# Token rows turned on TensorE, gathers first, and the weights loaded in three groups

## The reference

```
h = embed_matrix[x]                                   # x: (4, 1024) int32, embed_matrix: (50257, 192)
h = h + mamba_like(layernorm(h))                      # x@W_in, causal conv of 3, silu, cumsum*BC + xc*D, *silu(z), @W_out
h = h + routed_block(layernorm(h), ...)               # scores, 15% of the tokens attend, the others mix, then an FFN
h = h + memory_attention(layernorm(h), ...)           # 12 heads over the tokens and over 100 memory rows, gate alpha
h = h + ternary_ffn(layernorm(h), w1, g1, w2, g2)     # bitlinear -> gelu -> bitlinear
```

```
BC  = sum(B * C, axis=-1)
mkv = memory_features @ w_mem + b_mem                 # memory keys and values
weight_quant(w) = clip(round(w * s), -1, 1) / s,  s = 1 / max(mean(|w|), 1e-5)      # w1: (768, 192), w2: (192, 768)
```

## Time and profile before

| | us |
|---|---|
| median of 3 runs | 1982.28 |
| the runs | 1982.28, 1982.16, 1995.48 |
| the profiled execution | 1991.73 |
| its span, first to last instruction | 1989.9 |
| mean granted TensorE clock (share of full speed) | 0.878 |
| busy: PE, DVE, ACT, POOL | 1642.2, 1356.8, 971.2, 126.8 |

### The profile page before, as it was taken

One profiled execution on the slowest core, in us unless ns is written; L12 is line 12 of the kernel. 1 busy time (PEld: TensorE's weight loads), 2 busy tenths in 40 slices (PEclk: granted clock), 3 DMA queues, 4 the chain that ended last, 5 costly groups with the idle time before them and its releaser, 6 DMA issues.

```text
span 1989.9 us, 26444 instructions
## 1 busy us (share of the span) xinstructions
PE 1642.2 (83%) x9798; PEld 919.7 (46%) x9798; DVE 1356.8 (68%) x3076; ACT 971.2 (49%) x1383; POOL 126.8 (6%) x165
## 2 busy tenths in 40 slices
PE   0769878998999999964457898799999999999454
PEld 0348646654333333363243584656534333336323
DVE  4668663046889989677768477422588998984876
ACT  0422452124777777732532324330567777775153
POOL 5010000000000000005020100000000000000200
PEclk9977796998999999986568787899989999999656
DMA  6003210016010010001010312000510100100001
GB/s 149 1 1 112 68 44 0 1 35 187 25 32 25 25 32 25 1 1 32 0 33 0 99 45 67 13 0 1 179 60 25 32 25 27 30 9 1 0 0 32
DMA packets 53894, 73.39 MB, mean 37 GB/s; under 512 B 18712, under 2 KB 27205, under 8 KB 53767
## 3 DMA queue, kind: packets, MB, share of 16 engines
q1 hardware_dynamic: 52150, 68.54, 11.9%
q0 software_dynamic: 1616, 3.16, 0.7%
HBM read 38.51 MB, written 33.17 MB: 36 GB/s over the span
## 4 chain that ended last, share of the span: by engine, by line
PE 64%; DVE 26%; ACT 4%; issue 3%; DMA 2%; SPq 1%; POOL 0%; DVEq 0%; ACTq 0%
PE PV L905 9%; PE ST L889 8%; PE S L855 6%; PE ST L801 4%; PE ST L556 4%; PE MT L855 3%; PE PV L914 2%; DVE nmp L1529 2%; DVE Er L1605 2%; DVE st L1402 2%; PE S L812 2%; DVE R L1625 2%; DVE amax L1626 2%; PE ST L586 1%; PE S L850 1%
## 5 line engine op out<-in xcount | busy, mean ns | idle before, releaser
L1232 ACT ACTIVATE Er<-ST 128x1024 f32<-128x1024 f32 x384 | 377.1, 1021 | 106.2 <-PE ST L889 105.9
L1581 DVE TENSOR_REDUCE nmp<-S 128x1 f32<-128x512 f32 x514 | 337.7, 683 | 30.5 <-PE S L855 30.5
L889 PE MATMUL ST<-QS,KS 100*128 100x512 bf16 x768 | 218.0, 385 | 0.3
L905 PE MATMUL PV<-Er,V 128*17 128x512 f32 x1536 | 212.1, 602 | 0.0
L855 PE MATMUL S<-KS,QS 96*128 96x512 bf16 x514 | 183.3, 392 | 0.8
L1581 DVE TENSOR_REDUCE nmp<-MT 128x1 f32<-128x512 f32 x254 | 173.6, 683 | 13.5 <-PE MT L855 13.5
L855 PEld LDWEIGHTS S<-KS,QS 96*128 96x128 bf16 x514 | 48.2, 98 | 154.9 <-DVE nmp L1581 107.2
L450 POOL TENSOR_SCALAR tp<-mv 128x8 f32<-128x8 f32 x20 | 5.2, 258 | 1693.1 <-DVE mv L1406 1693.1
L1529 DVE TENSOR_REDUCE nmp<-S 128x1 f32<-128x512 f32 x120 | 77.5, 684 | 48.3 <-PE S L671 48.1
L889 PEld LDWEIGHTS ST<-QS,KS 100*128 100x128 bf16 x768 | 72.1, 99 | 64.2 <-ACT Er L1232 5.7
L855 PE MATMUL MT<-KS,QS 96*128 96x512 bf16 x254 | 99.4, 391 | 0.9 <-DVE nmp L1581 0.9
(11 more groups left out here) (386 smaller groups left out, 3210.9 us busy)
## 6 DMA issues: line engine op xcount, KB each, us to landing
KS<-scr_k SPq DMA_DIRECT2D x72, 192.0 KB, 2.7
scr_k<-R SPq DMA_DIRECT2D x16, 576.0 KB, 4.0
QS<-scr_q SPq DMA_DIRECT2D x48, 192.0 KB, 2.8
scr_k<-R SPq DMA_DIRECT2D x16, 384.0 KB, 4.6
QS<-scr_k SPq DMA_DIRECT2D x24, 192.0 KB, 2.4
scr_q<-R SPq DMA_DIRECT2D x8, 576.0 KB, 4.5
scr_k<-R SPq DMA_DIRECT2D x16, 192.0 KB, 5.2
scr_q<-R SPq DMA_DIRECT2D x8, 384.0 KB, 4.7
```

The costliest lines, as they stand in the source:

```text
L889: ins = nc.tensor.matmul(ST[i % 2][:, (kt % 2) * HALF:(kt % 2 + 1) * HALF], KS[0:KP + 4, k, kt * P:(kt + 1) * P], QS[0:KP + 4, k, half * H ...
L905: ins = nc.tensor.matmul(PV[row:row + VC, :], slots[h // H].V[:, kt, h % H, :], E[:, step % RING, (kt % 2) * HALF:(kt % 2 + 1) * HALF], st ...
L1232: A_(E[:, g, :], ST[i % 2][:, :], ACT.Exp).then_inc(s["exps"], 1)
L1581: v.tensor_reduce(nmp[:, u // 2, u % 2:u % 2 + 1], bank, AX.X, ALU.max).then_inc(s["reduced"], 1)
```

## The change

The change reorders the start of the kernel and one step of each pair.

- **Tokens.** SP loads the token numbers first, as 32 rows of 128 numbers. DVE turns the integers into floats, PE turns the 32 x 128 tile (with `ident`), and DVE writes the result as integers into `tok_i`. POOL waits for that and issues the gathers before most of its constants: eight for a, five for z, then a's inverse deviation, then z's last three and z's inverse deviation, then the remaining constants (`late_consts`).
- **Loads.** There are three semaphores: `early` (memory features, memory weight, w1, w2), `loaded` (input projection, convolution, columns, B and C) and `rest` (all others). PE waits for `early` before the memory products, for `loaded` before the first input projection, for `rest` before the first output projection.
- **Staging.** w1 and w2 are staged in the two buffers HS, and the memory weight in the buffer Er, in place of slot a's X, R and XT.
- **DVE.** Some of POOL's fills (vm, memt, splm, ones) and those of two PSUM banks are put at the start of DVE's list. Slot a's statistics come first; the split of the memory keys and w1's ternary passes stand between them and a's normalisation, w2's ternary passes before z's statistics. The fill of ksm, the rows of ones in XT and B*C (`late_fills`) stand between the first convolutions and the first scans.
- **Ternary weights.** PE turns them after the input projection of pair 0, in the four banks of D2, and ACT evicts them after the last SiLU of the convolution; PE waits for that (`wprep`) before the output projection.
- **Order within a pair, both pairs.** PE: turn a, project a (first half), turn z, project z; ACT accordingly.

```diff
-        wmem = slots[0].XT
-        w1 = slots[0].X[:, 0:FC, :]
-        w2 = slots[0].R[0:CH, 0:2 * F].rearrange("p (t f) -> p t f", t=2)
+        wmem = Er[0:CH + 1, 2720:2720 + 4 * D].rearrange("p (c n) -> p c n", c=2)
+        w1 = slots[0].HS[:, 0:FC, :]
+        w2 = slots[1].HS[0:CH, :, :].rearrange("p t d -> p (t d)").rearrange("p (t f) -> p t f", t=2)
+        tok_r = Er[0:NB * T, 3488:3488 + P].bitcast(I32)
+        tok_f = Er[0:NB * T, 3616:3616 + P]
...
@@ SP
+            sp.dma_start(tok_r, A["x"].rearrange("b (t p) -> (b t) p", p=P)).then_inc(s["tokens"], 16)
+            load(memn, A["L1_attn_memory_features"][0], "early")
+            load(wmem[0:CH, :, 0:2 * D], cm(A["L1_attn_w_mem"]), "early")
+            load(wmem[CH:CH + 1, 1, 0:2 * D], A["L1_attn_b_mem"].rearrange("(a n) -> a n", a=1), "early")
+            load(w1, cm(A["L1_ffn_w1"], P), "early")
+            load(w2, cm(A["L1_ffn_w2"]), "early")
+            load(win[:], cm(A["L0_attn_W_in"]), "loaded")
+            load(convw[:], A["L0_attn_conv_w"].rearrange("(c p) a k -> p c (a k)", p=CH), "loaded")
...
+            load(bmat[:], cm(A["L0_attn_B"]), "loaded")
+            load(cmat[:], cm(A["L0_attn_C"]), "loaded")
             load(wout[:], cm(A["L0_attn_W_out"]))
...
-            sp.wait_ge(s["pd"], 2)
+            sp.wait_ge(s["pd"], 3)
...
@@ POOL
-            g.dma_start(tok_i[:], A["x"].rearrange("b (t p) -> p (b t)", p=P), allow_slow_non_contiguous=True).then_inc(s["tokens"], 16)
...
-            g.wait_ge(s["tokens"], 16)
-            for o in slots:
-                gather(0, o)
+            g.wait_ge(s["tokens"], 18)
+            gather(0, a)
+            gather(0, z, range(0, 5))
+            inverse_deviation(0, a, 0)
+            gather(0, z, range(5, T))
+            inverse_deviation(0, z, 0)
+            late_consts()
...
@@ PE
-            pe.wait_ge(s["consts"], NCONST)
-            pe.wait_ge(s["filled"], 3)
-            pe.wait_ge(s["loaded"], LOADED)
+            pe.wait_ge(s["consts"], 1)
+            pe.wait_ge(s["tokens"], 17)
+            nc.tensor.transpose(ST[1][:, 0:NB * T], tok_f, ident[0:NB * T, 0:NB * T]).then_inc(s["pp"], 1)
+            pe.wait_ge(s["filled"], 1)
+            pe.wait_ge(s["early"], EARLY)
...
-                for o in slots:
-                    turn_norm(p, o, 0)
-                for c in range(2):
-                    for o in slots:
-                        inproj(p, o, c)
+                turn_norm(p, a, 0)
+                if p == 0:
+                    pe.wait_ge(s["loaded"], LOADED)
+                inproj(p, a, 0)
+                turn_norm(p, z, 0)
+                inproj(p, z, 0)
+                for o in slots:
+                    inproj(p, o, 1)
+                if p == 0:
+                    turn_ternary()
+                    pe.wait_ge(s["wprep"], 4)
+                    pe.wait_ge(s["rest"], OTHERS)
+                    pe.wait_ge(s["consts"], NCONST)
+                    pe.wait_ge(s["filled"], 3)
+                    pe.wait_ge(s["pa"], 5)
...
@@ ACT
             act.wait_ge(s["mw"], 96)
             for p in range(NPAIR):
-                for o in slots:
-                    evac(p, o, 0, o.XT)
-                for c in range(2):
-                    for o in slots:
-                        inproj(p, o, c)
-                    for o in slots:
-                        conv(p, o, c)
+                evac(p, a, 0, a.XT)
+                inproj(p, a, 0)
+                evac(p, z, 0, z.XT)
+                inproj(p, z, 0)
+                for o in slots:
+                    conv(p, o, 0)
+                for o in slots:
+                    inproj(p, o, 1)
+                for o in slots:
+                    conv(p, o, 1)
+                if p == 0:
+                    ternary()
+                    act.wait_ge(s["consts"], NCONST)
+                    act.wait_ge(s["filled"], 3)
...
@@ DVE
+            ve.wait_ge(s["tokens"], 16)
+            v.tensor_copy(tok_f, tok_r).then_inc(s["tokens"], 1)
+            ve.wait_ge(s["pp"], 1)
+            v.tensor_copy(tok_i[:], ST[1][:, 0:NB * T]).then_inc(s["tokens"], 1)
...
+            def late_fills():
+                link(v.memset(ksm[KP:KP + 4, :, :], 1.0))
+                v.memset(ksm[KP:KP + 2, :, :], 0.0).then_inc(s["filled"], 1)
+                for o in slots:
+                    v.memset(o.XT[CH:CH + 1, 1, :], 1.0).then_inc(s["pa"], 1)
+                ve.wait_ge(s["loaded"], LOADED)
+                link(v.tensor_tensor(bmat[:], bmat[:], cmat[:], ALU.mult))
+                link(v.tensor_reduce(cols[:, :, 6], bmat[:], AX.X, ALU.add))
...
+                if p == 0:
+                    ve.wait_ge(a.s["gathered"], 128)
+                    stats(p, a, a.U)
+                    split_memory()
+                    ternary(w1, w1q[:, 0:FC, :], P, 0)
+                    normalise(p, a, 0, a.U, a.rn)
+                    ternary(w2, w2q[0:CH, :, :], CH, 1)
+                    ve.wait_ge(z.s["gathered"], 128)
+                    stats(p, z, z.U)
+                    normalise(p, z, 0, z.U, z.rn)
...
                 for c in range(2):
                     for o in slots:
                         convolve(p, o, c)
+                    if p == 0 and c == 0:
+                        late_fills()
                     for o in slots:
                         gate(p, o, c)
```

More of the change, by code:

```diff
@@ L282, in build @@
         QR = ("qr0", "qr1", "qr2", "qr3")
-        loads = []
+        loads = {"early": 0, "loaded": 0, "rest": 0}
         a, z = slots
@@ L404, in _ @@
                 sp.wait_ge(o.s["stored"], NPAIR * 32 + 32)
-        LOADED = loads[0] * 16
-        NCONST = 14
+        EARLY, LOADED, OTHERS = loads["early"], loads["loaded"], loads["rest"]
+        NCONST = 9
         @block.gpsimd
@@ L464, in inverse_deviation, with gather @@
                 g.tensor_tensor(o.rnn[:], o.rnn[:], o.rn[:], ALU.mult).then_inc(o.s["rstd"], 1)
-            def gather(p, o):
-                for t in range(T):
+            def gather(p, o, tiles=range(T)):
+                for t in tiles:
                     b = 2 * p + o.x
@@ L481, in _ @@
                 g.wait_ge(s["qones"], p + 1)
-                for n in range(5):
+                for n in range(0 if p else 1, 5):
                     for o in slots:
@@ L1393, in _, with ternary @@
+            def ternary(w, q, n, c):
+                if c == 0:
+                    ve.wait_ge(s["pp"], 6)
+                    link(v.tensor_scalar(wsinv[:], PV[:, 0:2], 1.0 / (D * F), 1e-5, ALU.mult, ALU.max))
+                    link(v.reciprocal(wscale[:], wsinv[:]))
                 link(v.tensor_scalar(w, w, wscale[0:n, c:c + 1], MAGIC, ALU.mult, ALU.add))
```

153 lines of the change are left out of this document (68 added, 85 removed).

## The result

The changed kernel took 1968.17 us (median of 12 runs, 1964.36 to 1978.39), the kernel before, on the same chip, 1990.71 (12 runs, 1982.16 to 1995.48). The ratio is 0.9906, with a 95% interval of 0.9889 to 0.9923: a gain of 18.7 us (1990.7 x 0.0094; by the interval 15.3 to 22.1). The forecast was 1957 and a gain of 25.4. The later runs put the kernel before 8.4 us above the median of three that the forecast started from, so 11.2 us of difference in the time is made of 6.7 in the gain and 8.4 in the starting point, less 3.8, by which the two medians stand further apart (22.5) than the ratio says.

What follows compares the result with a forecast made beforehand. The start was taken as the bound: weight loads until 34.57 us, then serial preparation to the first scan at 84.53. Scan 27.2 us earlier, less 1.8 in pair 1, gives 25.4; 1982.3 - 25.4 = 1957 us, range 1950 to 1968.

Steps and rivals of the forecast that it cites:

- part 5: Pair 0 after its first scan: turning and evicting the ternary weights costs nothing; without DVE's second scan pass as cover, 5.15 us.
- port rival: Early gathers beside DVE's fills are held up at VectorE's port; slot a late by up to 10.7 us, 1967 us; chance 0.08.
- part 2: DVE's chain to a's first turn: PE turns from 29.8; memory keys' store costs nothing, 1 to 3 us if behind weights.
- the loads move the wait: Rival: memory keys' store or first loads come late, holding slot a back 3 to 8 us; 1960 to 1965; chance 0.12.
- the bounds' sum: Whole-kernel gain limits: up to 30 us with early gathers and free pair 1, down to 18 with slow tokens and other costs.
- part 3: Slot z at the start: first half normalised at 40.3, a's projection takes 6.9 us until 41.0, z evicted by 45.3.
- half-rate rival: PE's projections stay at 1.2 GHz in both pairs, 27.5 us more in each, 2012 us; chance 0.03.
- part 6: New order in both pairs: two bubbles of 0.9 us, pure loss of 1.8 us in pair 1, bounds 0 and 3.
- the clock column: Profile's granted clock, 1.00 for pair 0 from the start; by the skill's rule instead, the sum would be 1 to 2 us smaller.
- the new order in pair 1, 1.8 us: Pair 1: two eviction bubbles of 0.9 us each delay the scan; a slow-clock projection start adds up to 1.1 us.
- The price of the latest landing of z: Slot z's last gathers at the start: landing at the latest, they cost 1.6 us beyond a slack of 0.7 us.

Runs made afterwards that it cites:

- e1: Changed kernel with ScalarE's wait for the memory keys' store moved from before its first eviction to behind the first convolutions; ratio to the kernel before 0.9876.
- e2: Changed kernel with the late fills called before z's first convolution instead of after it; ratio to the kernel before 0.9892.
- e3: Changed kernel with the old order (both slots turned before a's projection) in pair 1 only; ratio to the kernel before 0.9907.
- e8: Changed kernel with the old order of turns and projections in both pairs; median 1970.93 us, ratio to the kernel before 0.9925.
- e9: Changed kernel run again, unedited; ratio to the kernel before 0.9911.
- e20: Changed kernel run again, unedited, beside e19 on the same chip; median 1966.52 us, ratio to the kernel before 0.9884.
- e15: Changed kernel with only 36 identity matmuls added on TensorE after the weight sums; median 1968.83 us, ratio to the kernel before 0.9878.
- e13: Changed kernel with the three edits and 36 identity matmuls on TensorE after the weight sums; ratio to the kernel before 0.9834.
- e14: The kernel of e13 once more, for one profile; first scan at 54.0 us, no whole time given.
- e19: The kernel of e13 again, beside the unedited changed kernel on one chip; median 1955.24 us, ratio to the kernel before 0.9818.
- e4: Changed kernel with the three edits together; ratio to the kernel before 0.9880.
- the three edits: Changed kernel with store's wait later, fills before z's convolution, old order in pair 1; mean 1964.7 us over 18 runs, changed kernel 1968.7.
- the identity matmuls: 36 matmuls of the identity, results unused, on TensorE after the weight sums; with the three edits, mean 1959.6 us over 10 runs.
- e6: Kernel with the three edits, and all eight gathers of z issued before a's inverse deviation instead of five; median 1966.41 us, ratio 0.9901.
- e7: Changed kernel with token numbers fetched the old way, by POOL in single elements; first scan 65.7 us against 63.1, no whole time given.

## Why the prediction was wrong, step by step

**Right, within 1.2 us.** Gathers at 5.20 (forecast 5.0); the statistics of a at 20.78 (21.2); POOL's inverse deviation at 25.85 (26.3); TensorE's first turn at 28.61 (29.8); z's statistics at 34.72 (34) and its normalisation at 39.72 (39.1); the fills 4.77 us from z's convolution to the scan (4.3), all on the path; the ternary weights hidden (part 5). The port rival was nearly empty: of the 16 first gathers one took 1.66 us and the very first 1.23, the rest 0.95.

**Failed: the store of the memory keys, "cost taken: nothing" (part 2).** The forecast let the weights be through at 27.4, from 6.8 MB and 268 GB/s, and gave the store the 1.8 us of landing that it had on an empty queue. The bytes were about right, for the 6.8 MB hold 1.49 of gathers: in the changed kernel 7.06 MB had moved by 32.2. The rate was not. 268 GB/s is that of three microseconds; from 2.0 to 32.2 the changed kernel's engines had a share of 1.07 and moved 233 GB/s, and they were full until 32.3. The store's issues took 4.63 us instead of 2.80 and its landing 6.0. The first eviction came at 34.53 instead of 30.9, 3.6 us late. e1 shows it by taking the wait away. How late it is varies: the six profiles in which nothing before the first eviction differs (changed, e2, e3, e8, e9, e20) have it at 31.3 to 35.3, and in e3, the earliest, the share had fallen to 0.54 by 30 to 31. It is the mechanism of the rival "the loads move the wait", which had 0.12, within the 3 to 8 us that it gave. The text had even named the price (1 to 3 us, if it queues behind weights) but left it out of the bounds' sum.

**Failed: "the projection takes half of 13.75, 6.9 us" (part 3).** It took 9.46, 2.6 us more: 0.2 because 16 matmuls by themselves take 7.08 at the full rate, and 2.4 for the slow start, by the 0.43 of a slow matmul some five or six of the 16. The half-rate rival came true for these alone, not for a pair. The bound for it stood under part 6 alone, as 1 to 2 us, and the forecast went by the clock column, which reads 1.00 there. That column was no evidence: TensorE had done nothing by then, and in the changed kernel it reads 1.00 too, over groups of 1.06 us. Only where the level falls after having risen, as in e15, does it show. The length of the matmuls is the reading to go by. e13, e14, e19 and e15 show that TensorE's work well ahead of the projection decides it, and where there is none, the moment of the rise is open (three fast, nine slow). Since turning z then ran at the full rate, 3.0 us instead of 4.3 from projection to projection, 1.3 came back.

Together: 3.6 late at the eviction, 0.2 between it and the projection, 2.6 in the projection, less 1.3, and 0.7 in z's convolution and the fills: 5.8 us, the scan at 63.12 instead of 57.3.

**Mis-sized: the new order in pair 1, 1.8 us.** It cost 3.3 at the scan (e3, e8, e4), 3.2 of it from the first turn on. The bubbles of the evictions are 0.7 of it, against 1.8; the clock is 2.0, against the 1.1 that the bound allowed without a row for it; the split of the projections, which the forecast did not have, is 0.5.

**Smaller readings.** The token numbers landed in 1.6 us (2.5 taken). In the kernel before the gathers did not wait for them, though their 7.5 us might suggest it: POOL's own constants released the first one,

```profile
14.14 1.09 POOL L469 DMA_INDIRECT U<-_L_tok_embed_matrix_dram,tok_i  x1 [0.71 <-POOL cnt L447]
```

and the change moved both out of the way. The price of the latest landing of z (8.0 us) is 2.3, not 1.6, by the forecast's own sum; it did not come to that.

**The starting point.** The forecast subtracted its gain from 1982.3, the median of three runs, where the profiled execution had 1991.7. With twelve runs the median is 1990.7.

The sign and the chain were right: 5.8 + 1.5 of 25.4 us were lost, 7.3, and the gain measured is 6.7 short.

**Open.** Why the three edits gave 4.0 us (standard error 1.9) of the 12 that their stages show. With the identity matmuls it was 9.1 (3.1), and all 28 runs together give 5.8 (1.8). The granted clock of the later stages in short bursts moves single spans by more than that, and what sets it there was not tried. Whether the identity matmuls bring anything to the whole time is open as well: by the first scan they bring nothing once the edits are in, and e15, which has them alone, has a ratio of 0.9878 against 0.9884 to 0.9911 without.

## What to carry to other kernels

When work is pulled to the front, every small transfer that it depends on now queues behind the bulk loads: take its landing from a row with a full queue, not from an empty one, and move the wait for it to its first reader. Take the rate of that queue over the whole load, too, and not from its best microseconds. After an idle TensorE take the length of the matmuls, not the clock column, and let the cheap short work have the slow microseconds. Before work is thrown away to raise the rate, look whether the faster matmuls are still on the path: here they were not once the other limits were gone. And price a change of one per cent by the stages that it touches: the stages that it doesn't touch may scatter by as much.

## What was not expected of the hardware

- A small store issued while the queue carries weights: 6.0 us to land instead of 1.8 (4.4 in e3, 7.5 in e6), and 4.63 us of issues for six instead of 2.80 (single ones 1.06, in the chain above); 2.81 in e1, e3 and e7.
- 16 KB of token numbers in single elements: 7.5 us to land in the kernel before, 11.2 in e7, with the first gather at 13.4; as 32 rows of 512 B 1.6 us, and with casts and a turn on TensorE the first gather at 5.2.
- The gather beside DVE's first ternary passes (tensor_scalar, 128x1152) took 1.62 to 1.66 us instead of 0.95 in most profiles, 1.11 to 1.30 in e14, e15 and e20; beside memsets, and beside the normalisation of a, it took 0.95.
- TensorE fell to the 1.2 GHz level about 1 us after it had resumed from 2.92 us of idle time, not in it (e15).
